# Causal attention inside a four-sequence layer kernel: values held as the matmul's weights, split probabilities streamed past them

## The reference

```python
q = (x @ Wq).reshape(S, 16, 64); k = (x @ Wk).reshape(S, 4, 64); v = (x @ Wv).reshape(S, 4, 64)
q, k = rope(q), rope(k)                    # 16 query heads, 4 key/value heads, 64 wide
scores = q @ k.T / 8, masked to key <= query
out = softmax(scores) @ v                  # per head, 1024 x 64
x = x + gate * (out.reshape(S, 1024) @ Wo)
```

## Time and profile before

| | |
|---|---|
| median of 3 runs | 2219.19 us |
| profiled execution, its own time | 2220.59 us |
| its span, first to last instruction | 2218.9 us |
| PE, weight loads, DVE, ACT, POOL busy | 86%, 76%, 57%, 30%, 21% |
| mean granted TensorE clock | 0.913 of full |

### The profile page before, as it was taken

How to read it: one execution, slowest core, us unless ns; L and a number is a source line. 1 busy time by engine, 2 the same in 40 slices (tenths; PEclk the granted TensorE clock), 3 DMA queues, 4 the chain that set the end, 5 groups by cost and what they waited for, 6 DMA issues and landing times.

```text
span 2218.9 us, 29750 instructions
## 1 busy us (share of the span) xinstructions
PE 1909.2 (86%) x11156; PEld 1683.8 (76%) x11156; DVE 1260.5 (57%) x2566; ACT 673.4 (30%) x1281; POOL 464.2 (21%) x799
## 2 busy tenths in 40 slices
PE   6868699999876879999976869999987687999997
PEld 4657598889755769889865668898976476988996
DVE  4597635552658844554358874545345886355435
ACT  1303233333321323333131323333322032333423
POOL 0051212211134111221015112212112411122101
PEclk8989879999998879999989887999999897899999
DMA  5400343230410152231050033233032005233204
GB/s 225 180 1 1 96 104 82 58 96 15 171 49 1 28 144 58 82 96 44 11 209 0 1 90 95 59 95 96 15 148 73 1 1 138 64 98 79 71 1 190
DMA packets 68639, 170.02 MB, mean 77 GB/s; under 512 B 9663, under 2 KB 24831, under 8 KB 64774
## 3 DMA queue, kind: packets, MB, share of 16 engines
q1 hardware_dynamic: 61190, 154.34, 23.2%
q10 hardware_dynamic: 7296, 13.63, 2.1%
HBM read 112.62 MB, written 45.63 MB: 71 GB/s over the span
## 4 chain that ended last, share of the span: by engine, by line
PE 59%; DVE 21%; issue 6%; DVEq 5%; DMA 3%; POOL 3%; ACT 2%; SPq 1%; POOLq 1%; ACTq 0%
PE ps L491 21%; PE ps L336 7%; DVE ps L1020 6%; PE ps L459 5%; PE ps L478 5%; PE ps L477 5%; PE ps L655 5%; PE ps L342 3%; PE ps L678 3%; DVE hrow L935 2%; DVE prod L1082 1%; DMA gate_scratch<-grow 1%; PE ps L502 1%; DVEq L1104 1%; DVE orow L1034 1%
## 5 line engine op out<-in xcount | busy, mean ns | idle before, releaser
L491 PEld LDWEIGHTS ps<-v,pT 128*128 128x128 f32 x4608 | 571.1, 199 | 13.4 <-ACT pT L757 1.9
L491 PE MATMUL ps<-v,pT 128*128 128x65 f32 x4608 | 562.5, 279 | 1.5 <-ACT pT L757 1.5
L1020 DVE CUSTOM_DVE_ANT_0 ps<-ps,mrow 128x128 f32<-128x128 f32 (+7 forms) x512 | 374.5, 785 | 294.5 <-PE ps L459 293.7
L757 ACT ACTIVATE pT<-ps 128x512 f32<-128x512 f32 (+3 forms) x768 | 334.9, 505 | 513.9 <-PE ps L478 503.8
L1248 POOL TENSOR_SCALAR_AFFINE_SELECT pT<-pT 128x128 f32<-128x128 f32 x512 | 146.3, 294 | 954.4 <-ACT pT L757 948.8
L459 PE MATMUL ps<-khl,qhh 128*128 128x512 f32 (+3 forms) x768 | 232.0, 389 | 74.5 <-DMA qhh<-work 33.6
L477 PE MATMUL ps<-qhh,khl 128*128 128x512 f32 (+3 forms) x768 | 277.7, 367 | 9.4 <-DVE orow L1034 6.3
L478 PE MATMUL ps<-q,k 65*128 65x512 f32 (+3 forms) x768 | 266.4, 359 | 0.0
L459 PEld LDWEIGHTS ps<-khl,qhh 128*128 128x128 f32 x768 | 133.6, 204 | 102.6 <-issue 51.0
L477 PEld LDWEIGHTS ps<-qhh,khl 128*128 128x128 f32 x768 | 152.3, 198 | 32.8 <-DVE orow L1034 8.4
L1030 DVE RECIPROCAL den<-ps 128x4 f32<-128x4 f32 x128 | 23.3, 182 | 269.8 <-PE ps L491 269.8
(11 more groups left out here) (164 smaller groups left out, 2511.6 us busy)
## 6 DMA issues: line engine op xcount, KB each, us to landing
qhh<-q_scratch SPq DMA_DIRECT2D x112, 256.0 KB, 4.2
q<-q_scratch SPq DMA_DIRECT2D x56, 256.0 KB, 4.7
q_scratch<-hrow SPq DMA_DIRECT2D x12, 1024.0 KB, 5.4
q_scratch<-work SPq DMA_DIRECT2D x12, 1024.0 KB, 4.8
sgn<-sgn_scratch SPq DMA_DIRECT2D x8, 1024.0 KB, 13.5
Kf<-kf_scratch SPq DMA_DIRECT2D x4, 2048.0 KB, 17.6
khl<-k_scratch SPq DMA_DIRECT2D x24, 256.0 KB, 5.9
in_w<-in_w_scratch SPq DMA_DIRECT2D x4, 1536.0 KB, 10.8
```

Of the source, the lines that this page charges most:

```text
L491: q = mm(ps[:, b, (i % 4) * (HD + 1):(i % 4 + 1) * (HD + 1)], pT[:, slot, i * P - lo:(i + 1) * P - lo], v1[:, g, j, :], start=j == 0, stop ...
L757: A(pT[:, n % PRING, 0:(c + 1) * HALF - lo], ps[:, b, 0:(c + 1) * HALF - lo], ACT.Exp, scale=SCALE)\
L1020: V.tensor_tensor_reduce(out=v, in0=v, in1=mrow[:, L - n:L], scale=1.0, scalar=-3e38, op0=ALU.add, op1=ALU.max, accum_out=mx[:, u % 2, i:i ...
```

## The change

`values` is turned round. The value rows, 65 columns with the ones, become the weights, split into `vhi` and `vlo`; the probabilities are streamed, split into `phi` and `plo`. Each block takes three products, hi*hi, lo*hi and hi*lo, of the block's whole width, and the output comes out already transposed: 64 values and the sum on 65 partitions, queries along the row. Two PSUM banks, 0 and 1, are kept for the two halves (`bk.low = 2`), so 6 are left in the ring.

ACT now computes the exp of each block twice, in full into one of three buffers (`FRING`) and as fp32r into `phi` (5 slots, `PRING`). POOL masks both. The difference, `plo`, is made by `score_low`, on POOL for the first 6 blocks of a head and on DVE for the last 6. ACT copies the output to `osum` (`summed`). The sums lie in a row; they are spread over 128 partitions by DMA (`load_sums`), inverted by DVE (`invert`), written to HBM, read back broadcast to 64 partitions (`spread_inverse`), and DVE multiplies the head's 64 x 1024 output by them (`scale`). `turn_outputs` and `normalise` are gone. All engines go through a head by its 12 blocks, PE with the values four blocks (`LAG`) behind the scores. After the last head the first two tile pairs with `wo` start on the heads that are ready.

The diff, cut to its core:

```diff
-GROUP_AT = {0: 1, GQ + 1: 2, 2 * GQ + 1: 3}
-PRING = 8
+GROUP_AT = {0: 1, GQ: 2, 2 * GQ: 3}
+PRING = 5
+FRING = 3
+BLOCKS = tuple((0, j) for j in range(4)) + tuple((1, j) for j in range(8))
+NBLK = len(BLOCKS)
+LAG = 4
+ROWS_AT = {0: (0, 1), 1: (2,), 2: (3,), 3: (4,), 4: (5,), 5: (6,), 6: (7,)}
+TURN_AT = 8
+POOL_LOW = BLOCKS[:6]
+DVE_LOW = BLOCKS[6:]
...
+            def values(u, c, j):
...
+                if j == 0:
+                    bk.take(pe, ("pv", u, c), until=(s["o_done"], NHALF * u + c + 1), at=c, counted=False)
...
+                if j * P >= c * HALF:
+                    pe.wait_ge(s["masked_done"], NT * u + j + 1)
+                else:
+                    pe.wait_ge(s["exp_done"], n + 1)
+                o = ps[0:HD + 1, c, lo - c * HALF:HALF]
+                high, low = phi[:, n % PRING, 0:hi - lo], plo[:, n % PRING, 0:hi - lo]
+                mm(o, vhi[:, g, j, :], high, start=j == 0, stop=False)
+                mm(o, vlo[:, g, j, :], high, start=False, stop=False)
+                pe.wait_ge(*low_made(n))
+                mm(o, vhi[:, g, j, :], low, start=False, stop=j == 4 * c + 3).then_inc(s["pv_done"], 1)
...
                 for u in range(HEADS):                                            # PE
+                    for n, (c, j) in enumerate(BLOCKS):
+                        score_cols(u, c, j)
+                        if u and n == 4 and u in GROUP_AT:
...
+                        if u + 1 < HEADS:
+                            for i in ROWS_AT.get(n, ()):
+                                score_rows(u + 1, i)
+                            if n == TURN_AT:
+                                turn_maxima(u + 1)
+                        if NBLK * u + n >= LAG:
+                            values(u if n >= LAG else u - 1, *BLOCKS[n - LAG])
...
             def exps(u, c, j):
...
+                if n >= PRING:
+                    act.wait_ge(s["pv_done"], n - PRING + 1)
+                if n >= FRING:
+                    act.wait_ge(*low_made(n - FRING))
+                A(full(n)[:, 0:hi - lo], ps[:, b, 0:hi - lo], ACT.Exp, scale=SCALE)
+                A(phi[:, n % PRING, 0:hi - lo], ps[:, b, 0:hi - lo], ACT.Exp, scale=SCALE)\
                     .then_inc(s["exp_done"], 1)
+
+            def summed(u, c):
+                act.wait_ge(s["pv_done"], NBLK * u + 8 * c + 4)
...
+                A(osum[:, u % 2, c * HALF:(c + 1) * HALF], ps[0:HD + 1, c, :], ACT.Copy).then_inc(s["o_done"], 1)
...
                 for u in range(HEADS):                                            # ACT
+                    for n, (c, j) in enumerate(BLOCKS):
+                        exps(u, c, j)
+                        if n == LAG and u:
+                            summed(u - 1, 1)
...
+                        if n == 8:
+                            summed(u, 0)
+                        if n == TURN_AT + 1 and u + 1 < HEADS:
+                            turn_maxima(u + 1)
...
+            def invert(u):
+                dve.wait_ge(s["sum_loaded"], 16 * (u + 1))
...
+                V.reciprocal(rden[:, u % 2, :], den[:, u % 2, :]).then_inc(s["inverse_done"], 1)
+
+            def scale(u):
+                dve.wait_ge(s["inverse_loaded"], 16 * (u + 1))
+                V.tensor_tensor(oT[u % 2 * HD:(u % 2 + 1) * HD, u // 2, :], osum[0:HD, u % 2, :], rb[:, :], ALU.mult)\
+                    .then_inc(s["oT_done"], 1)
...
                 for u in range(HEADS):                                            # DVE
+                    for n, blk in enumerate(BLOCKS):
...
+                        if w < HEADS:
+                            for i in ROWS_AT.get(n, ()):
+                                row_maxima(w, i)
+                        if n == 4 and u:
+                            invert(u - 1)
+                        if n == 6 and w < HEADS:
...
+                            negate(w)
+                        if n == 7 and k:
+                            low(k)
+                        if blk in DVE_LOW:
+                            score_low(u, *blk)
+                        if n == 9 and u:
+                            scale(u - 1)
...
                 for u in range(HEADS):                                            # POOL
+                    for n, (c, j) in enumerate(BLOCKS):
+                        if j * P >= c * HALF:
+                            mask(u, c, j)
+                        if (c, j) in POOL_LOW:
+                            score_low(u, c, j)
...
+                def load_maxima(u):
+
+                    sp.wait_ge(s["nmr_done"], u + 1)
+                    dma(q2[HD:HD + 1, u % 2, :].bitcast(F32), nmr[:, u % 2, :].bitcast(F32))\
+                        .then_inc(m_loaded(u)[0], 16)
+
+                def load_sums(u):
+
+                    sp.wait_ge(s["o_done"], NHALF * (u + 1))
+                    dma(den[:, u % 2, :], osum[HD:HD + 1, u % 2, :]).then_inc(s["sum_loaded"], 16)
+
+                def spread_inverse(u):
+
+                    r = u % 2
+                    sp.wait_ge(s["inverse_done"], u + 1)
+                    dma(inverse_scratch[r:r + 1, :].rearrange("a (p k) -> p (a k)", p=P), rden[:, r, :])\
+                        .then_inc(s["inverse_stored"], 16)
+                    sp.wait_ge(s["inverse_stored"], 16 * (u + 1))
+                    sp.wait_ge(s["oT_done"], u) if u else None
+                    dma(rb[:, :], inverse_scratch[r:r + 1, :].broadcast_to([HD, L])).then_inc(s["inverse_loaded"], 16)
...
                 for u in range(HEADS):                                            # SP
...
+                    if u:
+                        sp.wait_ge(s["exp_done"], NBLK * u)
+                        if u + 1 < HEADS:
+                            load_query_low(u + 1)
+                    if u + 2 < HEADS:
+                        load_query(u + 2)
...
+                    if u:
+                        load_sums(u - 1)
+                    if u + 1 < HEADS:
+                        load_maxima(u + 1)
+                    if u:
+                        spread_inverse(u - 1)
```

More of the change, by code:

```diff
@@ L221, in flat_split, with full @@
             return split_of(k).rearrange("p a e n -> p (a e) n").bitcast(F32)
+        osum = work[0:HD + 1, :, :].rearrange("p (u c) n -> p u (c n)", u=2)
+        def full(n):
+            r = n % FRING
+            return pT[:, r, :] if r < FRING - 1 else mix[:, 4:6, :].rearrange("p k n -> p (k n)")
         def stored_at(k):
@@ L625, in _ @@
-                    for j in range(4):
-                        score_cols(u, 1, j)
-                    b = bk.take(pe, ("pv", u, 0), until=(s["o_done"], 2 * u + 1))
-                    for i in range(4):
-                        if i == 3 and w < HEADS:
-                            for k in range(3):
-                                score_rows(w, k)
-                        q = values(u, 0, i, b)
-                    q.then_inc(ready[b], 1)
-                    if w < HEADS:
-                        for k in range(3, 4):
-                            score_rows(w, k)
@@ L637, in _ @@
-                    for j in range(4, NT):
-                        score_cols(u, 1, j)
-                        if w < HEADS:
-                            score_rows(w, j)
-                    b = bk.take(pe, ("pv", u, 1), until=(s["o_done"], 2 * u + 2))
-                    for i in range(4, NT):
-                        if i == 6 and w < HEADS:
-                            turn_maxima(w)
-                        q = values(u, 1, i, b)
-                    q.then_inc(ready[b], 1)
-                turn_outputs(HEADS // 2 - 1)
@@ new lines, in _, with attended @@
+                for n in range(NBLK - LAG, NBLK):
+                    values(HEADS - 1, *BLOCKS[n])
+                def attended(t, u, b, some):
+                    for q in some:
+                        i = mm(ps[:, b, u * D:(u + 1) * D], oT[:, q, (t + u) * P:(t + u + 1) * P], wo[:, q, :],
+                               start=q == 0 and (u == 0 or t >= 4), stop=q == HEADS // 2 - 1 and (u == 1 or t >= 4))
+                    return i
+                pe.wait_ge(s["oT_done"], HEADS - 2)
+                first = [(t, bk.take(pe, ("out1", t))) for t in (0, 2)]
@@ L649, in _ @@
+                for t, b in first:
+                    for u in range(2):
+                        attended(t, u, b, range(HEADS // 2 - 1))
+                pe.wait_ge(s["oT_done"], HEADS)
+                for t, b in first:
+                    attended(t, 0, b, (HEADS // 2 - 1,))
+                    attended(t, 1, b, (HEADS // 2 - 1,)).then_inc(ready[b], 1)
+                bk.low = 0
+                for t in (4, 6):
                     b = bk.take(pe, ("out1", t))
-                    pe.wait_ge(s["oT_done"], HEADS - 1 + t // 4)
@@ L653, in _ @@
                             route()
[L654 to L656 removed]
+                        i = attended(t, u, b, range(HEADS // 2))
                     i.then_inc(ready[b], 1)
```

273 lines of the change are left out of this document (127 added, 146 removed).

## The result

| | before | after |
|---|---|---|
| median of the timed runs, us | 2220.49 (2216.77 to 2221.84, 4 runs) | 2460.66 (2455.05 to 2469.44, 4 runs) |
| ratio to before, 95% interval | 1 | 1.1082 (1.1049 to 1.1115) |
| span of the profiled execution, us | | 2462.2 |
| mean granted clock of PE | 0.913 | 0.88 |
| first score product of sequence 1, us | 267.81 | 262.67 |

The change makes the kernel 11% slower. The forecast was 2418 us, range 2300 to 2560; the time is 43 us above it and inside the range. One run of all those reported here (2262.12 us, of `e4_before_rows_first`) was in a slower state, at a granted clock of 0.896, and is left out of its ratio.

A forecast was written before the change was run, and what follows sets the result against it. PE bounds the kernel before; after the change, a DMA chain once a head was to set a 20.6 us cycle against 16.0. That adds 49.4 us a sequence, 197.6 for four, to 2220.6: 2418 us, range 2300 to 2560.

The forecast's parts named there:

- The wait that is added: Once a head `scale` on DVE waits for the broadcast inverses, stopping ACT and PE; cycle 20.6 us against 16.0; chance 0.68.
- part A: From one maxima copy until block 10's difference is there, through store and broadcast of the inverses: 8.1 us, bounds 7.3 to 11.9.
- Part B: From block 10's difference to the next maxima copy, through the sums' DMA, `invert` and row maxima: 12.5 us.
- The cycle: From one head's maxima copy to the next: 20.6 us against 16.0.
- PE: what goes and what comes: PE's value products: 7.85 us and transposes of 0.45 go, 6.35 come, saving 1.95 us a head.
- The sum: Attention stage per sequence: 329.9 us for 280.5, so +49.4, and +197.6 for four sequences.
- head 0's copy to head 1's: In each sequence, first maxima copy to the second: B and 1.0, 13.5 us.
- The projections in heads 4 and 8: They delay row block 5 and all behind it, 5.65 us less a little each: 11 for both.
- What costs nothing: Last head's chain, 10.4 us, hidden beside 12.2 us of `wo` products; also `value_low` and SP's three more DMAs a head.
- Rival 1: The wait is hidden and PE stays the bound: 14.0 us a head, 2096 us; chance 0.07.
- Rival 2: DVE and POOL take turns: 14.9 us a head, about 16.5 with changeovers, 2254 us; chance 0.13.
- Rival 3: PE's clock stays at half, so its 12.7 us a head become 25.4: 2687 us; chance 0.12.

The follow-up runs named there:

- e4_before_rows_first: The kernel before plus one line: ACT waits for the first head's second half of rows before its second stores; 2220.96 us, ratio 0.9997.
- e1_swap: The changed kernel with SP issuing `spread_inverse(u-1)` ahead of `load_maxima(u+1)`; 2282.69 us, ratio to before 1.0297.
- e5_no_chain: The changed kernel without `load_sums`, `spread_inverse` and `invert`; `scale` multiplies by a rotary table row, outputs not normalised; 2173.31 us, ratio to before 0.9788.
- e7_best: `e6_late_high` with row maxima, turn and `negate` one block earlier and `scale` two later; 2168.88 us, ratio to before 0.9770.
- e6_late_high: `e3_both` with the next keys' high and low parts written in blocks 3 and 4 of the next head; 2174.10 us, ratio to before 0.9798.
- e3_both: The changed kernel with `spread_inverse` issued ahead of `load_maxima` and `invert` moved from block 4 to 6; 2211.93 us, ratio to before 0.9951.
- e9_no_rows_wait: `e6_late_high` without ACT's wait for `first_rows1` ahead of its second stores; 2183.90 us, ratio to before 0.9834.

## Why the prediction was right, and where it was off

**The wait that is added: right.** `scale` waits 4.4 us in the mean and ACT and PE stand behind it, as forecast. In the cycle shown, part A: 8.1 us forecast, 8.0 measured (300.93 to 308.93). Part B: 12.5 and 12.6. The cycle: 20.6 and 20.6. That it fits to the tenth is luck in part, for the terms were off in both directions. In B it took 4.9 us to the sums' DMA for 4.1, then 2.0 for 2.4, and 5.7 for the 6.0 of the rest. Of the signs, two came out otherwise: PE has no idle stretch of 5 us (in part A it idles for 3.1 us in all, not some 6), and `invert` waits 2.9 us in the mean, not 1 to 2. The view of DMA issues of the kernel after:

```profile
mix<-inverse_scratch SPq DMA_DIRECT2D x64, 256.0 KB, 3.6
...
den<-work SPq DMA_DIRECT2D x64, 4.0 KB, 2.0
...
inverse_scratch<-rden SPq DMA_DIRECT2D x64, 4.0 KB, 1.5
```

The store took 1.5 us for the 2.2 taken (the bound from below was 1.9, which the row undercuts), the broadcast 3.6 for 3.3, the sums 2.0 for 2.2. `e1_swap` shows that the cause is the place in SP's queue, as the prediction named it.

The Trainium skill, "DMA: Bandwidth & Descriptors", section on the anatomy of one DMA, has about 2.0 us plus the bytes at 436 GB/s, for transfers that GpSimd issues, which gave an estimate of 7.2 us for part A. Here SP issues them, and the 256 KB broadcast, for which that makes 2.6 us, took 3.6, and the 4 KB store 1.5. So the trace does not agree and the measurement decides; for the broadcast the bounds from the rows were nearer.

**PE: what goes and what comes: right.** The starts of the value products in the timeline of the kernel after:

```profile
600.72 0.39 PE L528 MATMUL ps<-phi,vhi 128*65 128x512 f32 x1
600.94 0.39 PE L529 MATMUL ps<-phi,vlo 128*65 128x512 f32 x1
601.17 0.40 PE L531 MATMUL ps<-plo,vhi 128*65 128x512 f32 x1
```

0.22 to 0.23 us apart, forecast 0.235. The 14.0 us a head that follow were reached by no kernel; 15.0 in `e5_no_chain` and 14.4 in `e7_best` are the nearest. In `e5_no_chain` a head's first score still waits for the maxima DMA, 37.8 us in all in 56 heads. The forecast did not hang on this, for in its cycle PE has time to spare.

**The sum: in sequence 1, 15.4 us too little, and 5.1 too much before it.** Against the terms of the prediction:

| term | forecast | measured | |
|---|---|---|---|
| start of the attention stage | 267.81 | 262.67 | -5.1 |
| head 0 to its copy | 14.5 | 16.7 | +2.2 |
| head 0's copy to head 1's | 13.5 | 21.6 | +8.1 |
| 13 cycles and the two projections | 278.8 | 285.5 | +6.7 |
| part A, head 15 and the rest to `wo` | 23.1 | 21.5 | -1.6 |

The other sequences differ a little. In all four the attention stages are 57 us longer than forecast (62 to 65 us each over before, for 49.4), and the parts ahead of them are 12 us shorter than before (5.1, 1.1, 4.1 and 1.6). That makes 46 us, the distance from 2418 to the 2463.96 us of the profiled execution. Three terms were mis-sized:
- *Head 0's copy to head 1's* was called B and 1.0, as if nothing else happened in head 1. But ACT has `high(5)` ahead of head 1's exponentials, and it waits for the store out of `hrow`. The two places that do it, `split_of` and the wait on `rope_stored` in `high`, are part of the change, though not of its core as shown; the prediction read the loss of a buffer without asking who had used the second one. The view of waits of the kernel after has it twelve times, 5.6 us in the mean, and its chain in order of time has the store for 4.83 us in this head. `e6_late_high`, which moves it, took 3.7 us from the same head in `e3_both`; the rest of the 8.1 was not taken apart:

```profile
ACT hrow L765 <- DMA q_scratch<-hrow: 67.5, 12, 6.8
```

```profile
280.39 4.83 DMA q_scratch<-hrow
```

- *The projections in heads 4 and 8* were 11 us for both, from the matmuls alone. Heads 4, 5, 8 and 9 are 18.4 us longer than a cycle each. In heads 5 and 9 the same wait stands again; how much of the excess it is, and what the rest in heads 4 and 8 is, was not taken apart.
- *The start of the stage* was costed at nothing. It came 5.1 us earlier in sequence 1; the added wait on ACT alone makes it 4.5 earlier in `e4_before_rows_first`.

**What costs nothing: right.** The products with `wo` in the kernel after run on without a stop beside the last head's chain, 21.12 us against the 20.91 of before:

```profile
608.00 21.12 PE L663 MATMUL ps<-wo,oT 128*128 128x256 f32 x96
```

**Rival 1, the wait hidden: fell,** for the reason given against it. `e3_both` and `e6_late_high` come near to it once the two issues have changed places and `invert` comes later, though with 15.3 and not 14.0 us a head.

**Rival 2, DVE and POOL take turns: seen, but not the bound.** The timeline of the kernel after:

```profile
279.05 1.27 POOL L1322 TENSOR_TENSOR oT<-oT 128x512 f32<-128x512 f32 x1
279.12 1.75 DVE L1072 TENSOR_TENSOR plo<-mix,phi 128x512 fp32r<-128x512 f32 x1 [0.43 <-POOL mix L1306]
...
301.77 0.65 POOL L1304 TENSOR_SCALAR_AFFINE_SELECT phi<-phi 128x128 fp32r<-128x128 f32 x1
```

A 512-wide difference takes 1.75 us beside a POOL operation, where the earlier trace rows has 0.69; a mask 0.65, which is 0.30 elsewhere. The Trainium skill, "SBUF — State Buffer", section on the two separate sides, says that the two engines lock their shared ports for a whole instruction, and these rows agree. But heads of 15.0 us in `e5_no_chain` and 14.4 in `e7_best` are shorter than the 16.5 that the prediction gave this rival. Laid over each other, POOL's operations and DVE's differences and `scale` cover 13.5 us of a head of 14.4 in `e7_best` and 14.3 to 14.7 of a plain cycle in the kernel after, near the 14.9 of the prediction. What was too much is the 1.6 us for changeovers, and this second bound lies close under the best heads.

**Rival 3, the clock stays low: a part.** The view by windows of the kernel after, beside the cycle above:

```profile
308.00:312.00 4.00, 2.88 (x10) 2.34 (x11) 3.84 (x13) 1.76 (x6) 1.93 (x5) 0.69 0.41 140
312.00:316.00 4.00, 4.00 (x12) 2.92 (x11) 1.17 (x4) 2.53 (x5) 3.03 (x6) 0.50 0.55 119
316.00:320.00 4.00, 3.77 (x21) 2.67 (x20) 3.45 (x8) 2.83 (x7) 1.29 (x1) 0.96 0.00 0
```

After PE's idle time in part A the clock is at the lower level (1.2 GHz) for most of 8 us, 12 matmuls where the window behind it has 21, and back at the upper. That is more than the 0.4 us that the prediction put in. PE is busy for 12.2 of part B's 12.6 us at a mean granted clock of 0.73, and the 0.8 us that B's first piece has too much may be the clock's; this is argued and not shown. Of the 4 us stretches from 60 us on, 93 of 600 have a busy PE at under 0.75 after, against 48 of 539 before and 31 of 526 in `e6_late_high`. The clock does not set the loss, since the swap alone took 178 us off; how many of the 240 us are its own, no run separates.

## What to carry to other kernels

A DMA queue is served in order, and an issue that waits holds up all behind it: write down for every issue when its data are ready, and put the one whose data come first ahead. The change lost 240 us, and changing the order of two lines on SP gave back 178 of them. When waits sit in one cycle, taking away one is worth only its part until the others are gone too, so undo them together before giving up the change: with all its arithmetic and DMAs it is 2.3% faster than before in `e7_best`, once the orders are right. Of such a gain a part is the added wait on ACT and not the turned product: `e6_late_high` is 2.0% faster with it, `e9_no_rows_wait` 1.7% without, with intervals that overlap. And where a buffer is dropped from a ring, look up every user of the one that is left.

## What the runs showed of the hardware

- Small DMAs on SP's queue landed after 1.5 us (4 KB from SBUF to HBM), 2.0 (4 KB spread over partitions) and 3.6 (256 KB broadcast to 64 partitions), medians of 64 each in the kernel after.
- PE can be busy for 4.00 of 4.00 us at a granted clock of 0.50 in four windows in a row, as from 1960 to 1976 us in `e4_before_rows_first`. An earlier start then need not bring an earlier end.
- Where an operation of DVE and one of POOL overlapped, one of the two took over twice as long in the rows shown (0.69 to 1.75 us on DVE, 0.30 to 0.65 on POOL).
